# Six float32 convolution taps, two (later four) of them in three float32r products each, with the experts' weights on VectorE and several steps moved

## What is computed

```python
x = x + tanh(g_xattn[0]) * conv_ref(layernorm(x), ctx, weight)
x = x + tanh(g_ffn[0])  * moe_ref(layernorm(x), router_w, router_b, A, Bm)

# conv_ref: B,C,T = 16,128,1024, O = 128, K = 3
sim = [cos(e[t], e[t-1]), 1, cos(e[t], e[t+1])]        # over channels, per position
att = repeat(sim, C, axis=1)                            # 384 rows, in blocks of 128
inp = stack([pad(f)[:, :, k:k+T] for k in range(3)], axis=2).reshape(B, 3*C, T)
out = einsum('bit,oi->bot', inp * att, weight.reshape(O, 3*C))

# moe_ref: N = 2048 tokens, D = 1024, E = 8 experts, R = 16
w  = scatter of the two largest softmax(x @ router_w.T + router_b), divided by their sum
hw = einsum('nd,erd->ner', x, A) * w[:, :, None]
out = einsum('ner,eor->no', hw, Bm) * 0.5
```

## Time and profile before

| | |
|---|---|
| runs | 217.45, 217.52, 215.83 us (median 217.45) |
| the profiled execution | 216.01 us, span 214.3 us |
| granted TensorE clock | 1.00 throughout |
| busy share of the span | PE 96%, DVE 79%, ACT 56%, POOL 53%, weight loads 60% |
| prologue (0 to about 57 us) | PE with short waits; batches 0 to 2 |
| batches 3 to 14 (about 57 to 199 us) | PE without idle time |
| last batch (199 to 214.3 us) | a chain over DVE, ACT and PE, then the last store |

### The profile page before, as it was taken

One profiled execution on the slowest core, in us unless ns is written; L12 is line 12 of the kernel. 1 busy time (PEld: TensorE's weight loads), 2 busy tenths in 40 slices (PEclk: granted clock), 3 DMA queues, 4 the chain that ended last, 5 costly groups with the idle time before them and its releaser, 6 DMA issues.

```text
span 214.3 us, 4481 instructions
## 1 busy us (share of the span) xinstructions
PE 205.5 (96%) x1450; PEld 127.7 (60%) x1450; DVE 168.2 (79%) x430; ACT 119.8 (56%) x228; POOL 112.9 (53%) x206
## 2 busy tenths in 40 slices
PE   8999999998999999999999999999999999999973
PEld 8885546475564647565656646464756565646662
DVE  3366896966989796998979698977788888787664
ACT  4678377866956573765656474746347454331320
POOL 4357555697768676475949357774440414131210
PEclk9999999999999999999999999999999999999999
DMA  6999560140252526151615222232205020202024
GB/s 177 356 369 314 212 195 3 34 169 3 98 199 98 196 99 199 44 196 57 234 62 195 95 107 101 98 99 98 101 0 196 2 101 2 98 0 101 0 99 196
DMA packets 14072, 26.79 MB, mean 125 GB/s; under 512 B 1250, under 2 KB 9570, under 8 KB 14050
## 3 DMA queue, kind: packets, MB, share of 16 engines
q1 hardware_dynamic: 14050, 26.51, 35.0%
HBM read 18.12 MB, written 8.39 MB: 124 GB/s over the span
## 4 chain that ended last, share of the span: by engine, by line
PE 88%; ACT 3%; DVE 3%; POOL 2%; issue 2%; DVEq 0%; ACTq 0%; POOLq 0%
PE conv_ps L1033 37%; PE hidden_ps L1084 13%; PE xT_ps L1043 6%; PE hidden_ps L962 5%; PE sim_ps L1022 5%; PE out_ps L1102 4%; PE out_ps L1103 3%; PE out_ps L1104 3%; PE conv_ps L1126 3%; POOL rinv L397 2%; PE xT_ps L975 2%; PE out_ps L1093 2%; PE xT_ps L1006 1%; PE out_ps L1119 1%; PE conv_ps L1054 1%
## 5 line engine op out<-in xcount | busy, mean ns | idle before, releaser
L1033 PE MATMUL conv_ps<-pt,wT 128*128 128x512 f32 x186 | 96.2, 601 | 0.2 <-DVE pt L732 0.2
L732 DVE TENSOR_TENSOR pt<-xn,sim_ps 128x512 f32<-128x512 f32 x96 | 60.2, 680 | 2.3 <-PE sim_ps L1022 1.8
L535 ACT ACTIVATE xT<-xT_ps 128x512 f32<-128x512 f32 x31 | 18.5, 597 | 37.1 <-PE xT_ps L1043 36.9
L1084 PEld LDWEIGHTS hidden_ps<-aT,xT 128*128 128x128 f32 x248 | 31.9, 190 | 7.1 <-issue 7.0
L1084 PE MATMUL hidden_ps<-aT,xT 128*128 128x136 f32 x248 | 33.7, 279 | 0.0
L1033 PEld LDWEIGHTS conv_ps<-pt,wT 128*128 128x128 f32 x186 | 30.4, 196 | 5.5 <-issue 3.5
L397 POOL TENSOR_TENSOR rinv<-nmax,minus_half 128x8 f32<-128x8 f32 x16 | 27.8, 1741 | 10.1 <-DVE nmax L669 10.1
L528 ACT ACTIVATE xn<-xt,offset,rs 128x1024 f32<-128x1024 f32 x16 | 19.9, 1244 | 8.0 <-POOL offset L408 8.0
L739 DVE TENSOR_TENSOR x<-conv_ps,xt 128x512 f32<-128x512 f32 x31 | 21.3, 688 | 2.2 <-PE conv_ps L1033 1.4
L388 POOL TENSOR_TENSOR qp<-qp 128x1024 f32<-128x1024 f32 x8 | 19.1, 2383 | 4.5 <-DVE qp L647 3.9
L1043 PEld LDWEIGHTS xT_ps<-wide,x 128*128 128x128 f32 x124 | 15.1, 140 | 10.3 <-issue 7.5
(11 more groups left out here) (150 smaller groups left out, 312.9 us busy)
## 6 DMA issues: line engine op xcount, KB each, us to landing
xt<-x SPq DMA_DIRECT2D x16, 512.0 KB, 3.4
out<-x SPq DMA_DIRECT2D x15, 512.0 KB, 2.6
et<-ctx SPq DMA_DIRECT2D x14, 514.0 KB, 5.7
aT_in<-expert_aT SPq DMA_DIRECT2D x1, 544.0 KB, 7.7
et<-ctx SPq DMA_DIRECT2D x2, 257.0 KB, 2.8
bm_in<-expert_b SPq DMA_DIRECT2D x1, 512.0 KB, 5.8
out<-x SPq DMA_DIRECT2D x2, 256.0 KB, 2.6
et<-ctx SPq DMA_DIRECT2D x1, 385.5 KB
```

Source lines behind the costliest of these rows:

```text
L535: nc.scalar.activation(xT[:, n % 2, 4 * h:4 * h + 4, :].rearrange("p c n -> p (c n)"), xT_ps[:, :], ACT.Copy).then_inc(xT_out, 1)
L732: nc.vector.tensor_tensor(pt[:, i, :], xn[:, n % 2, h * HALF + t:(h + 1) * HALF + t], sim_ps[:, t, :], ALU.mult).then_inc(mod_done, 1)
L1033: nc.tensor.matmul(conv_ps[h][:, :], wT[:, t * P:(t + 1) * P], pt[:, i, :], start=(t == 0), stop=(t == TAPS - 1)).then_inc(tap_done, 1)
L1084: last = nc.tensor.matmul(h_ps, xT[:, n % 2, c, :], aT[:, c, :], start=(c == 0), stop=(c == KC - 1))
```

## The change

- **Split taps.** In batches 3 to 9 the taps `i = 2, 5` (the third of each half), in batches 10 to 15 the taps 1, 2, 4 and 5 (not the second half of batch 15) are done as three float32r matmuls, `wT_lo x pt_hi`, `wT_hi x pt_hi`, `wT_hi x pt_lo`. ACT makes `pt_hi` from `pt` (`modulated_high`), POOL makes `pt_lo = pt - pt_hi` (`modulated_rest`). That is 14 and 22 taps, 36 in all.
- **Experts' weights** (`topf`, `ga`, `gb`, `gate`) and `hw` are made on DVE, between the three `modulate` of the next batch. POOL does none of them any more.
- **Product and folds.** DVE's `product(n + 6)` stands right behind `token_variance(n - 1)` and no longer at the loop's end; `product(6)` is POOL's. Contexts 4 and 5 are folded as well; POOL's `fold` of context `n + 5` stands between the subtractions of batch `n`.
- **Prologue.** Seven keep-warm matmuls for eleven; the mean of the experts' rows by three additions on DVE (`add_expert_rows`) and one matmul; group 1's sums are transposed into another bank; loads, PE, ACT and DVE steps in another order.
- **End.** `experts_out(13, 1)` goes behind the last `experts_in`; PE adds the input for the quarters 1 and 3 of the last batch, ACT brings them out and issues the last half's store; the stores of batches 13 and 14 go by halves.

```diff
-WARM_UP = 11
+WARM_UP = 7
-FOLDED = 8
+FOLDED = (4, 5, *range(8, 16))
+SPLIT = {n: (1, 2, 4, 5) if n >= 10 else (2, 5) for n in range(3, 16)}
+ADDED_ON_PE = (1, 3)
-ON_POOL = (3, 4, 5)
+ON_POOL = (3, 4, 5, 6)
...
         @block.gpsimd
...
+            def modulated_rest(k):
+                if is_split(k):
+                    pool.wait_ge(pt_hi_done, splits_up_to(k))
+                    if is_split(k - STEPS):
+                        pool.wait_ge(tap_done, k - STEPS + 1)
+                    nc.gpsimd.tensor_tensor(pt_lo[:, split_slot(k), :], pt[:, k % STEPS, :],
+                                            pt_hi[:, split_slot(k), :].bitcast(F32), ALU.subtract).then_inc(pt_lo_done, 1)
...
             product(4)
+            fold(4)
             product(5)
+            fold(5)
...
                 token_rstd(n - 1)
-                weigh_experts(n - 1)
-                hidden(n - 1)
+                modulated_rest(STEPS * n + 4)
+                modulated_rest(STEPS * n + 5)
+                if n in SUMMED and SUMMED[n] in FOLDED:
+                    fold(SUMMED[n])
                 if n + 2 < B:
                     feature_rstd(n + 2)
-                if n in SQUARED:
-                    fold(SQUARED[n])
+                if n + 1 < B:
+                    modulated_rest(STEPS * (n + 1) + 1)
+                    modulated_rest(STEPS * (n + 1) + 2)
...
         @block.scalar
+            def modulated_high(k):
+                if is_split(k):
+                    act.wait_ge(mod_done, k + 1)
+                    if is_split(k - STEPS):
+                        act.wait_ge(tap_done, k - STEPS + 1)
+                    nc.scalar.activation(pt_hi[:, split_slot(k), :], pt[:, k % STEPS, :], ACT.Copy).then_inc(pt_hi_done, 1)
...
         @block.vector
                 if n > 2:
                     token_variance(n - 1)
+                    if n in SQUARED:
+                        product(SQUARED[n])
...
-                if n + 1 < B:
-                    for k in range(TAPS):
+                for k in range(TAPS):
+                    take(weigh)
+                    if n + 1 < B:
                         modulate(STEPS * (n + 1) + k)
+                take(weigh)
...
         @block.tensor
+                if is_split(k):
+                    pe.wait_ge(wT_lo_done, 1)
+                    weight, j = slice(t * P, (t + 1) * P), split_slot(k)
+                    pe.wait_ge(pt_hi_done, splits_up_to(k))
+                    nc.tensor.matmul(conv_ps[h][:, :], wT_lo[:, weight], pt_hi[:, j, :], start=(t == 0), stop=False)
+                    nc.tensor.matmul(conv_ps[h][:, :], wT_hi[:, weight], pt_hi[:, j, :], start=False, stop=False)
+                    pe.wait_ge(pt_lo_done, splits_up_to(k))
+                    nc.tensor.matmul(conv_ps[h][:, :], wT_hi[:, weight], pt_lo[:, j, :], start=False,
+                                     stop=(t == TAPS - 1)).then_inc(tap_done, 1)
```

More of the change, by code:

```diff
@@ L159, in ffn_ps, with is_split, splits_up_to, split_slot @@
             return last_out_ps.get((n, h), out_ps[:, :])
-        means_ps = out_ps[:, 0:ER + E]
+        means_ps = out_ps[:, P:P + ER + E]
         gates_ps = sim_ps[:, 0, 0:2]
+        def is_split(k):
+            n, i = k // STEPS, k % STEPS
+            return i in SPLIT.get(n, ()) and (n, i // TAPS) != (B - 1, 1)
+        def splits_up_to(k):
+            return sum(is_split(j) for j in range(k + 1))
+        def split_slot(k):
+            return SPLIT_TAPS.index(k % STEPS)
         def quarter(w):
@@ L639, in _ @@
             hidden_hi(B - 1)
+            for w in ADDED_ON_PE:
+                act.wait_ge(ffn_done, 2 * B - 1 + w)
+                nc.scalar.activation(x1[:, G - 1, quarter(w)], quarter_ps[w], ACT.Copy).then_inc(last_out, 1)
+            act.wait_ge(out_done, 2 * B)
+            act.wait_ge(last_out, 2)
+            nc.scalar.dma_start(out[B - 1, :, half(1)], x1[:, G - 1, half(1)]).then_inc(last_stored, 16)
         @block.vector
@@ L798, in finish_last, with add_expert_rows, weigh_experts @@
                                         ALU.add).then_inc(out_done, 1)
-            def some(of, count):
-                for _ in range(count):
-                    next(of, None)
-            def weigh_last():
-                n, i = B - 1, (B - 1) % 2
-                dve.wait_ge(topi_done, B)
+            def add_expert_rows():
+                dve.wait_ge(aT_in_done, 16)
+                nc.vector.tensor_tensor(aT_sum[:, :, :], aT_in[:, 0:4, :], aT_in[:, 4:8, :], ALU.add).then_inc(aT_added, 1)
+                yield
+                dve.wait_ge(aT_added, 1)
+                nc.vector.tensor_tensor(aT_sum[:, 0:2, :], aT_sum[:, 0:2, :], aT_sum[:, 2:4, :], ALU.add).then_inc(aT_added, 1)
+                yield
+                dve.wait_ge(aT_added, 2)
+                nc.vector.tensor_tensor(aT_sum[:, 0, :], aT_sum[:, 0, :], aT_sum[:, 1, :], ALU.add).then_inc(aT_added, 1)
+                yield
+            def weigh_experts(n):
+                i = n % 2
+                dve.wait_ge(topi_done, n + 1)
                 nc.vector.tensor_copy(topf[:, i, :], topi[:, i, 0:2]).then_inc(topf_done, 1)
-                dve.wait_ge(weights_done, 2 * B)
-                dve.wait_ge(topf_done, B)
+                yield
+                dve.wait_ge(weights_done, 2 * (n + 1))
+                dve.wait_ge(topf_done, n + 1)
                 for j, target in enumerate((ga, gb)):
@@ L857, in _ @@
             take(chain)
+            adds = add_expert_rows()
+            take(adds)
+            take(chain, 5)
             residual(0, 0)
-            take(chain, 5)
+            take(adds)
+            rows_low(1)
+            take(adds)
+            modulate(STEPS)
             residual(0, 1)
-            rows_low(1)
-            for k in range(TAPS):
-                modulate(STEPS + k)
-            token_stats(0, 0)
+            modulate(STEPS + 1)
+            modulate(STEPS + 2)
             dve.wait_ge(mean_w_done, 1)
@@ L867, in _ @@
                                     ALU.subtract).then_inc(aT_done, 1)
+            token_stats(0, 0)
+            for k in range(TAPS, STEPS):
+                modulate(STEPS + k)
             token_stats(0, 1)
             token_variance(0)
-            for k in range(TAPS, STEPS):
-                modulate(STEPS + k)
             residual(1, 0)
@@ L878, in _ @@
                 modulate(2 * STEPS + k)
-            product(6)
+            weigh = weigh_experts(0)
+            take(weigh, 4)
             residual(1, 1)
@@ L1203, in _ @@
                 spread_similarities(n, 1)
+                tap(STEPS * n)
                 if n in TURNED:
@@ L1225, in _ @@
                     passed += 1
+                tap(STEPS * n + 5)
                 if n in SUMMED:
@@ L1236, in _ @@
             transpose_last(0)
+            experts_in(B - 1, 0)
+            transpose_last(1)
+            experts_in_last()
             experts_out(B - 3, 1)
-            transpose_last(1)
-            experts_in(B - 1, 0)
-            experts_in_last()
             experts_out(B - 2, 0)
+            for w in ADDED_ON_PE:
+                add_last(w)
+            transpose_hidden(B - 1)
             experts_out(B - 2, 1)
-            transpose_hidden(B - 1)
             for w in range(4):
```

196 lines of the change are left out of this document (104 added, 92 removed).

## The result

The changed kernel takes 250.32 us (median of 4 runs, 248.35 to 253.93) against 216.64 us before (4 runs). The ratio is 1.153, 95% interval 1.140 to 1.165; ratios here leave out executions that fell in a slower state of the core, here the one of 253.93. The forecast was 226, its range 210 to 241. The direction was right; the loss is more than three times as large as forecast. The profiled execution took 248.35 us, span 246.6 us.

What follows compares the result with a forecast made beforehand. PE was taken as the bound, DVE next with about 1.2 us in hand. From 216.0 us: batches 3–9 +6.8, 10 +0.8, 11 +1.0, 12–14 +1.8, 15 -0.3, end -0.8, giving 225.3, median 226; range 210 to 241.

Steps and rivals of the forecast that it cites:

- I take the hold for steps with two SBUF inputs: POOL reads of SBUF hold DVE steps with two SBUF inputs, for anything from nothing to the POOL step's full length.
- rival 3: Every SBUF step of DVE is held, casts and `ga` too; `topf` waits to the fold's end; median 241 us, chance 0.18.
- the sum: Adding up of step times and waits, by batch and for head and end: +9.3 us on 216.0, giving 225.3.
- `gate`, on which the forecast put 0.64 us: DVE step 2.98 us behind the logits, held to the fold's end at 3.62; batch becomes 11.8 us, 0.6 more.
- Rivals 1, 2 and 4: POOL never holds DVE: 212.7 us, chance 0.30; PE stays the bound: 208.4, 0.10; partial hold: about 217, 0.10.
- The head: Prologue: matmul savings taken back by one held addition, so 0, from -2 (no hold) to +1.5 us (both held).
- The 1.9 us that fewer matmuls were to save: In the prologue, PE time saved by one matmul for the means, fewer keep-warm matmuls and two folds: 1.9 us.
- DVE's own loop, 11.18 us in the sum: DVE's batch with product and weights, before POOL's holds: 11.18 us against 11.21 before, so no gain.
- DVE follows with about 1.2 us in hand: In batch 7 DVE's logits wait 1.22 us for PE's `hidden_ps`, read as DVE's slack behind PE.
- The 0.70 us of a triple and 0.16 of a split: On PE a float32r triple takes 0.70 us against 0.86; 36 splits save 5.8 us if PE stays the bound.
- `ve` was held to the product's end as forecast: POOL's `ve`, between variance and logits, ends 0.05 us behind DVE's product; the logits begin 0.65 later.
- -0.8 forecast: Kernel's end: one triple behind the last `experts_in`, quarters on PE spare DVE; -0.8 us, from -0.3 to -1.2.

Runs made afterwards that it cites:

- p1_probe: Kernel of its own without the computation, pairing a long POOL instruction with a short DVE one; a two-column cast beside POOL's 2.34 us addition took 1.95 us.
- a1_fold_late: Changed kernel with POOL's fold back at the end of POOL's loop; 232.49 us, ratio 1.076 to the kernel before.
- e2: c1 with two more waits in POOL's prologue: product(4) for the three additions, product(6) for ga and gb of batch 0; 224.51 us, ratio 1.040.
- c1: a1_fold_late with topf made by two casts of one column each instead of one of two; 227.95 us, ratio 1.056.
- g1_no_split: e2 without split taps, all taps in float32; 220.75 us, ratio 1.025.
- b3_weights_only: Kernel before with only topf, ga, gb, gate and hw of batches 1 to 14 moved to DVE, between the modulates; 222.15 us, ratio 1.027.
- h2: h1 with taps 1 and 2 of batches 11 to 15 split on top; 214.87 us, ratio 0.993.
- b2: Kernel before with only DVE's product moved behind the variance; 216.31 us, ratio 1.003.
- h1: Kernel before with the change's end alone; 214.89 us, ratio 0.993.

## Why the prediction was wrong

**The bound and the lock.** That PE led, with DVE next, and that POOL's reads would hold DVE, was right. The step that failed is "I take the hold for steps with two SBUF inputs". The hold takes casts and scalar steps from SBUF to SBUF as well, so it was rival 3 whose mechanism came true (chance 0.18): in batches 3, 4, 6, 7 and 9 `topf`, at 1.21 us behind the logits (1.28 in the sum), waits to the fold's end. In the chained batches 5 and 8 it is `rest`, 2.29 us, which the sum let wait 0.85 for the subtraction; it started 0.45 behind the logits for the 0.39 reckoned, but 1.41 behind POOL's subtraction, and the fold had begun. In batch 10 `topf` took 1.27 us, to the end of the second subtraction, where rival 3 had it wait for the fold's end. `gate`, on which the forecast put 0.64 us, waits nowhere, because `topf` has waited before it. Rivals 1, 2 and 4 fell with p1_probe and a1_fold_late.

**Rival 3 said 241, and 250 was measured.** Two terms were short.
- The head, put at 0 with a bound of +1.5, was +5.6 by the variance of batch 1. Both additions were held, 1.4 and 1.5 us too long, and `ga` and `gb` of batch 0 too, a meeting that I hadn't looked for; the two waits of e2 brought 4.1 back against c1. About 1.6 is the fall of the clock from 12 to 16 us, which the prediction didn't name. The 1.9 us that fewer matmuls were to save is seen in no run: with the new head the variance of batch 1 is never earlier than before.
- DVE's own loop, 11.18 us in the sum, is 11.78 in g1_no_split, where nothing is held. Two waits are missing in the sum:

```profile
106.74 0.29 DVE L838 TENSOR_TENSOR hwT_lo<-out_ps,hwT_hi 128x128 fp32r<-128x128 f32 x1 [0.19 <-ACT hwT_hi L600]
...
107.92 0.17 DVE L720 TENSOR_SCALAR nmax<-xT_ps 128x8 f32<-128x8 f32 x1 [0.29 <-PE xT_ps L1054]
```

Before, the product stood right ahead of `hwT_lo`, and DVE waited at neither. The sum took the product out of that place at its full 1.21 us; 0.48 of it came back as these waits; the last 0.1 is small differences, the second cast of `topf` among them. The wait for the reciprocal (0.70 in g1) was in the sum. One slip in the sum changes nothing: by its own rows the last `simp` comes at 2.24 us and not at 2.27.

For the weights without the product's move (b3_weights_only, +6 us without any hold) the term that failed is "DVE follows with about 1.2 us in hand". Of that wait of the logits 0.92 us would have been spent on the reciprocal anyway, as the row beside it (97.50, waiting for POOL) already showed, and at the end the wait for PE was part of a circle.

**Split taps.** The 0.70 us of a triple and 0.16 of a split were near (h2, 0.27 for two in its last full batch), and worth nothing here: PE wasn't the bound, and the subtractions held DVE. Leaving the splits out gained 3.8 us. POOL's subtraction takes 1.28 us for the 1.19 estimated.

**Product.** `ve` was held to the product's end as forecast (1.06 us), and in the kernel before it costs nothing measurable (b2). With the weights on DVE it uncovers the two waits shown above.

**End.** -0.8 forecast, -1.1 measured (h1).

**The sum, by the runs:** from 250.3 the fold's place takes 17.8 us, the form of `topf` 4.5, the head's meetings 3.4, the splits 3.8, to 220.75. What is left to 215.8 is about 5 us. By the traces of g1 and of the kernel before (4.5 us apart in span) it is 2.0 in the head, mostly the clock, 3.8 from the variance of batch 1 to that of batch 14, less 1.3 at the end. Of the 3.8, 3.5 are lost up to the variance of batch 11, where DVE's loop with a product takes 11.78 us. It isn't b3's 6.3 for the weights less the end's 1.1, though the numbers nearly fit: from batch 11 to 14 b3 loses 2.7 us by its trace, and g1 0.3. This ladder is a chain of single steps, each on top of the last. The fold's 17.8 includes PE's lower granted clock (0.945 in the changed kernel, 0.978 in a1): by these means PE stood at the lower level for some 27 us and 10 us, so at most 8.5 us of the 17.8 can be the clock's, an estimate that takes PE as the bound all that time.

## What to carry to other kernels

Before a step goes to DVE, look at what POOL reads at that time: any DVE instruction that has two SBUF inputs, or casts or scales from SBUF to SBUF, can wait to the end of a POOL addition, subtraction or copy that started first, with two columns as with 72. If the step can't be moved, change its form (an operand or the output in PSUM, one column at a time), and measure it in a pair of instructions first. And a wait of an engine counts as slack only if nothing else waits behind it and it isn't an arc of the circle that sets the period: find what the engine would wait for next.

## What the runs showed that I had not expected

- A cast of one column beside a 2.34 us POOL addition took 0.14 us, of two columns 1.95.
- A POOL memset of 128x1024 (0.95 us) holds a DVE cast and a scalar step (0.54 us each) but not a step with two inputs (0.16).
- POOL's power of 8 columns held neither a step with two inputs nor a cast (0.16 us both), though it ran for 1.65 us.
- Weights on POOL together with subtractions and fold cost as much as the hold: 253.9 us for 250.3.
